# The value mix of two local attention phases, computed transposed on 64x64 parts of TensorE

## The chip, the cores and the metric

One Trainium2 chip, one of its cores. The metric is the time of one execution on the device in microseconds (us); lower is better. The kernel is written directly for the engines: TensorE (PE), VectorE (DVE), ScalarE (ACT), GpSimd (POOL) and SyncE (SP) each have a program of their own, and semaphores tie them together.

## The reference

A four-layer decoder over `x` (32 sequences of 64 tokens, 128 features) with attentions, cross attentions and feed-forward blocks. The change touches the local attention of `_L0_ffn_ref`, which is computed twice (depth 2), each time followed by a gated feed-forward block. With 64 tokens in a sequence and a window of 64, each sequence is one window, and it comes down to this:

```
qkv = shift_token(x) @ wqkv                      # 128 -> 3 * 512
q, k, v = heads of 64 features, 8 heads
q, k = rotary(l2norm(q) * q_scale), rotary(l2norm(k) * k_scale)
sim = einsum('bhid,bhjd->bhij', q * 8, k)        # 64 x 64 for each sequence and head
attn = softmax(where(causal, sim, -max), axis=-1)
out = einsum('bhij,bhjd->bhid', attn, v)
x = x + out.reshape(b, n, 512) @ wo
```

## The kernel before, in words

The 2048 token rows are 16 tiles of 128 rows (two sequences each). A turn takes two tiles, called streams 0 and 1, so a phase has 8 turns (`TURNS`). The two local attentions are the phases F0_ATTN and F1_ATTN. They run through `piped3` (L272): a body works on three turns at once, a tail (scores, softmax, mix, output), a middle (norms and rotation of queries and keys) and a front (load, transpose, projection). Each phase has two bodies without a tail, six full ones (tail, middle, front) in a hardware loop, a seventh tail without a front, and an eighth tail alone.

Every engine walks its part of `three` in the order in which it is written; there is no planner. For a full body:

- DVE (`three` of `wide_vector`, L1112): for the middle the sums of squares (L1045, L1048) and the scaling to unit length (L1052); for the tail the softmax shift (L378, L380); rotation of the middle's stream 0 (L1034 to L1036); for the tail the row sums (L1067), their reciprocals (L1072) and `normal_heads` (L1080), which reads the mixed heads of PSUM, multiplies them by one over the row sum and writes them to `mixed_heads`; rotation of stream 1; the residual sum (L335).
- PE (`three` of `wide_tensor`, L910): for the tail the transposes of queries and keys (L820), the values (L838), the scores (L813, 16 matmuls for a stream, on 64x64 parts of the array); for the front the transposes of `xs` (L304) and the projection (L827); then for the tail `turn_probs_pe` (L397: four transposes L401 for a stream, 128x128, two heads each), `mix` (L841), `turn_heads` (L850, four transposes L853), `output` (L857, four accumulating matmuls for a stream).
- ACT (`three` of `wide_scalar`, L995): queries (L954), values (L961, two copies for a stream), for the front L312 and L314, exp (L388), squares (L1011), the copy of the turned probabilities (L395) and of the turned heads (L969).
- POOL (`three` of `wide_pool`, L764): for the middle the power -1/2 (L768, twice), stage of `xs` (L299), L780, and for each stream the addition that completes the rotation (L783), as soon as DVE has rotated that stream.

The helper `mm` (L285) records all matmuls, so PE's matmuls show as L285 and are told apart by tiles and shapes. A float32 matmul has two records in the profile, a transpose one.

The mix multiplies, for head pair `c` and sequence `b`, the turned probabilities (128 rows: the keys of two heads; 64 columns: queries) by `values64`, which holds the values of both heads in block diagonal form with zeros between. Its result has queries in partitions, so `turn_heads` transposes it before `output`.

`mixed_heads` shares its memory with `probs`, `headsT` with `probsT`. All are parts of one SBUF tensor, `arena`, and PSUM shows as `ps`.

## Time and profile before

| | |
|---|---|
| time, median of 3 runs | 1894.24 us (1893.24 to 1895.31) |
| the profiled execution's own time | 1894.01 us |
| its span, first to last instruction | 1892.2 us |
| busy: PE, DVE, ACT, POOL | 78%, 64%, 42%, 39% |
| TensorE clock granted, mean | 0.896 of full speed |

The busy shares are means over 15 phases with different limits, and say little about the two phases that change. The timeline below lists merged instructions: start in the span, length from the first to the last of the group, engine, line, operands, count, and in square brackets how long the engine sat idle before and what ended that. "PE" rows are matmuls. The change applies to the stretches from 288 to 449 us and from 547 to 706 us.

### The profile page before, as it was taken

What the parts mean: (1) busy time and instruction counts of PE and PEld (TensorE: products, weight loads), DVE (VectorE), ACT (ScalarE), POOL (GpSimd) and SP (SyncE); (2) the same over time, 40 slices, a digit from 0 to 9 for tenths busy, and PEclk for the clock granted to TensorE, in tenths of its full rate; (3) what the DMA queues carried; (4) which work ended last, traced back from release to release, by engine and by line L of the source; (5) the groups of instructions that cost most, each with busy time, mean ns of one, the idle gap of its engine ahead of it and who ended that gap; (6) DMA issues with size and microseconds to landing.
All of it is one profiled execution on the core that took longest, in us unless ns stands there. A gap on an engine that the chain in (4) does not pass through costs nothing.

```text
span 1892.2 us, 42651 instructions
## 1 busy us (share of the span) xinstructions
PE 1479.7 (78%) x16082; PEld 1042.8 (55%) x16082; DVE 1216.5 (64%) x2671; ACT 789.4 (42%) x1513; POOL 730.5 (39%) x961
## 2 busy tenths in 40 slices
PE   4979967877878878799999786928988688898830
PEld 2656735556745556466666554925555567565520
DVE  4974658784467765657575586435788245698867
ACT  1542315554545544354545353514555123355520
POOL 2541125641155532324242362544566111356620
PEclk9988869998889997999999897868999599899975
DMA  7000000000000000000000000211000000000000
GB/s 297 0 1 0 0 1 1 0 1 19 0 1 0 0 6 6 17 1 0 0 0 0 1 0 23 50 52 77 0 1 1 0 1 0 1 0 2 0 2 22
DMA packets 14384, 27.69 MB, mean 15 GB/s; under 512 B 3830, under 2 KB 10998, under 8 KB 13544
## 3 DMA queue, kind: packets, MB, share of 16 engines
q1 hardware_dynamic: 13064, 24.15, 3.6%
q0 software_dynamic: 1248, 2.56, 0.6%
q8 instruction: 48, 0.79, 0.2%
q14 instruction: 24, 0.20, 0.0%
HBM read 23.10 MB, written 3.60 MB: 14 GB/s over the span
## 4 chain that ended last, share of the span: by engine, by line
PE 33%; issue 28%; DVE 17%; POOL 16%; ACT 4%; POOLq 1%; SPq 0%; DMA 0%; DVEq 0%; ACTq 0%
PE ps L285 27%; DVE maxima L378 6%; POOL arena L783 4%; DVE arena L380 3%; PE ps L401 3%; POOL inv_norm L768 3%; ACT arena L388 2%; POOL arena L754 2%; POOL arena L465 2%; DVE heads_out L677 2%; POOL arena L758 2%; POOL rstd L319 1%; PE ps L820 1%; DVE arena L1034 1%; POOL arena L1662 1%
## 5 line engine op out<-in xcount | busy, mean ns | idle before, releaser
L285 PE MATMUL ps<-arena 128*32 128x64 f32 (+6 forms) x7797 | 380.1, 281 | 45.0 <-ACT arena L395 11.8
L285 PEld LDWEIGHTS ps<-arena 64*64 64x64 f32 (+4 forms) x7797 | 252.7, 133 | 159.2 <-issue 98.5
L465 POOL TENSOR_TENSOR arena<-arena,w_const 128x1024 f32<-128x1024 f32 x96 | 182.3, 1901 | 151.1 <-DVE arena L662 64.9
L378 DVE TENSOR_REDUCE maxima<-ps 128x16 f32<-128x1024 f32 (+1 forms) x144 | 158.4, 1100 | 101.4 <-PE ps L285 100.1
L319 POOL TENSOR_TENSOR rstd<-var_eps,minus_half 128x1 f32<-128x1 f32 x160 | 87.7, 565 | 287.4 <-DVE var_eps L361 287.4
L388 ACT ACTIVATE arena<-arena 128x1024 f32<-128x1024 f32 (+1 forms) x144 | 138.5, 962 | 135.0 <-DVE arena L380 134.5
L401 PE MATMUL ps<-w_const,arena 128*128 128x128 f32 x1024 | 139.0, 280 | 46.9 <-ACT arena L388 46.7
L380 DVE TENSOR_TENSOR arena<-ps,maxima 128x1024 f32<-128x1024 f32 (+1 forms) x144 | 159.2, 1106 | 5.0
L401 PEld LDWEIGHTS ps<-w_const,arena 128*128 128x128 f32 x1024 | 115.9, 143 | 69.9 <-ACT arena L388 62.5
L395 ACT COPY arena<-ps 128x1024 f32<-128x1024 f32 (+1 forms) x144 | 129.6, 916 | 29.5 <-PE ps L401 28.7
L783 POOL TENSOR_TENSOR arena<-arena 128x1024 f32<-128x1024 f32 x32 | 77.2, 2413 | 135.4 <-DVE arena L1036 135.4
L677 DVE RECIPROCAL heads_out<-ps 128x128 f32<-128x128 f32 x96 | 91.3, 951 | 56.8 <-PE ps L285 56.5
L304 PE MATMUL ps<-w_const,xs 128*128 128x128 f32 x192 | 63.8, 341 | 79.4 <-POOL xs L299 69.9
L304 PEld LDWEIGHTS ps<-w_const,xs 128*128 128x128 f32 x192 | 28.3, 148 | 136.7 <-issue 69.8
L768 POOL TENSOR_TENSOR inv_norm<-sq_floor,minus_half 128x16 f32<-128x16 f32 x32 | 92.5, 2907 | 16.4 <-DVE sq_floor L1048 14.9
L617 ACT COPY arena<-ps 64x128 f32<-64x128 f32 x192 | 49.1, 256 | 114.4 <-PE ps L285 113.3
L954 ACT COPY arena<-ps 128x1024 f32<-128x1024 f32 x48 | 48.6, 1012 | 115.3 <-PE ps L820 115.3
L820 PE MATMUL ps<-w_const,arena 128*128 128x128 f32 x512 | 68.5, 281 | 25.9 <-POOL arena L783 20.2
L820 PEld LDWEIGHTS ps<-w_const,arena 128*128 128x128 f32 x512 | 56.9, 143 | 36.8 <-POOL arena L783 20.0
L961 ACT COPY arena<-ps 64x512 f32<-64x512 f32 (+1 forms) x96 | 69.3, 721 | 13.5 <-PE ps L285 11.3
L754 POOL TENSOR_TENSOR arena<-arena 128x1024 f32<-128x1024 f32 x16 | 37.4, 2355 | 95.8 <-DVE arena L1036 95.8
L1052 DVE TENSOR_TENSOR arena<-ps,inv_norm 128x1024 f32<-128x1024 f32 x32 | 39.2, 1224 | 52.5 <-POOL inv_norm L768 52.5
(280 smaller groups left out, 3090.7 us busy)
## 6 DMA issues: line engine op xcount, KB each, us to landing
experts<-in_pack_moe SPq DMA_DIRECT2D x2, 4180.0 KB, 19.8
w_a<-in_pack_a SPq DMA_DIRECT2D x1, 2080.0 KB, 16.9
w_fa<-in_pack_fa SPq DMA_DIRECT2D x2, 1024.0 KB, 11.5
moe_out<-arena SPq DMA_DIRECT2D x5, 256.0 KB, 2.3
w_fg<-in_pack_fg SPq DMA_DIRECT2D x2, 537.0 KB, 11.8
ctxT<-in_ctxT SPq DMA_DIRECT2D x1, 1024.0 KB, 7.5
moe_in<-state SPq DMA_DIRECT2D x1, 1024.0 KB, 5.5
out<-state SPq DMA_DIRECT2D x1, 1024.0 KB, 5.1
```

The source lines that it names most:

```text
L285: return nc.tensor.matmul(o, lhsT, rhs, start=start, stop=stop, skip_group_check=True)
L319: nc.gpsimd.tensor_tensor(rstd[s][:, :], var_eps[s][:, :], minus_half[:, 0:1], ALU.pow)\
L378: nc.vector.reduce_max(mx, sc, X_AXIS).then_inc(signal["max_ready"], 1)
L380: nc.vector.tensor_tensor(probs(s)[:, 0:heads * S].rearrange("p (a h k) -> p a h k", a=2, h=half), sc, mx.unsqueeze(3).broadcast_to([P, 2, ...
L388: nc.scalar.activation(probs(s)[:, 0:n], probs(s)[:, 0:n], ACT.Exp, scale=scale)\
L395: nc.scalar.copy(probsT(s)[:, 0:n], pair(s, 2)[:, 0:n]).then_inc(signal["probsT_ready"], 1)
L401: last = nc.tensor.transpose(pair(s, 2)[:, j * P:(j + 1) * P], probs(s)[:, j * P:(j + 1) * P], ident)
L465: nc.gpsimd.tensor_tensor(keys_wide(s).rearrange("p (b h t) -> p b h t", b=SEQS, h=8), key8(s).rearrange("p (b t) -> p b t", b=SEQS).unsqu ...
L677: nc.vector.reciprocal(heads_out[s][:, :], bank(s, 1, P, 2 * P)).then_inc(signal["sums_inverted"], 1)
L768: nc.gpsimd.tensor_tensor(inv_norm[s][:, :], sq_floor[s][:, :], minus_half[:, :], ALU.pow).then_inc(signal["norms_inv"], 1)
L783: nc.gpsimd.tensor_tensor(roped(s), roped(s), rope_swapped(s), ALU.add)\
L820: last = nc.tensor.transpose(pair(s, first)[:, j * P:(j + 1) * P], source[:, j * P:(j + 1) * P], ident)
```

## The change

It replaces three steps of the tail in both phases:

- `normal_heads` goes. `normal_probs` on DVE multiplies the probabilities in `probs` by one over their row sums, in place, before they are turned. `turn_probs_pe` now waits for that (`heads_normal`) where it waited for exp (`probs_ready`).
- `mix` becomes `mix_turned`: for every pair `c`, sequence `b` and head `par` of the pair one matmul with the 64x64 block of values as the stationary side and the turned probabilities as the moving side. It reads partitions `par*64` to `par*64+63` and writes the same partitions of PSUM bank 2. The result has features in partitions, so it needs no transpose: `turn_heads` and its four transposes for a stream go, and `heads_mixed` on ACT copies PSUM to `headsT` (the counterpart of L969).
- The values are kept densely in `values_plain`, one copy (`values_whole`) for a stream in place of two (L961).

The third wide phase, L1_ATTN, keeps the old functions.

```diff
-                        turn_probs_pe(tail, heads)
-                        for s in STREAMS:
-                            mix(tail, s)
-                    if tail:
-                        for s in STREAMS:
-                            turn_heads(tail, s)
+                        turn_probs_pe(tail, heads, ready="heads_normal")
+                        for s in STREAMS:
+                            mix_turned(tail, s)
                         for s in STREAMS:
                             output(tail, s)
...
+                def mix_turned(t, s):
+                    t.wait("probsT_ready", s, alone=True)
+                    for c in range(half):
+                        for b in range(SEQS):
+                            for par in range(2):
+                                rows, cols = slice(par * S, (par + 1) * S), slice(c * P + b * S, c * P + (b + 1) * S)
+                                last = mm(bank(s, 2)[rows, cols], values_plain(s)[rows, b, c, :],
+                                          probsT(s)[rows, cols])
+                    last.then_inc(signal["mixed"], 1)
...
+        def values_plain(s):
+            return probsT(s)[:, 512:1024].rearrange("p (b c d) -> p b c d", b=SEQS, c=4)
...
+                def values_whole(t):
+                    for s in STREAMS:
+                        t.wait("v_projected", s)
+                        nc.scalar.copy(values_plain(s).rearrange("p b c d -> p (b c d)"), bank(s, 2))\
+                            .then_inc(signal["values_ready"], 1)
+
+                def heads_mixed(t):
+                    for s in STREAMS:
+                        t.wait("mixed", s)
+                        nc.scalar.copy(headsT(s)[:, 0:half * P], bank(s, 2)).then_inc(signal["headsT_ready"], 1)
...
+                def normal_probs(t):
+                    for s in STREAMS:
+                        t.wait("sums_inverted", s)
+                        per_head = probs(s)[:, 0:heads * S].rearrange("p (h k) -> p h k", h=heads)
+                        nc.vector.tensor_tensor(per_head, per_head,
+                                                inv_sum[s][:, 0:heads].unsqueeze(2).broadcast_to([P, heads, S]),
+                                                ALU.mult).then_inc(signal["heads_normal"], 1)
...
                     if tail:
                         row_sums(tail)
-                        normal_heads(tail)
+                        normal_probs(tail)
                     if middle:
                         unit_rotated(middle, 1, tail)
```

PE's program in the loop body of F0_ATTN, from the turned probabilities to the loop's end, first before (L401 transposes of probabilities, `arena 64x128` the mix, L853 transposes of heads, `w_fa,arena` the output):

```order
L401 MATMUL ps<-w_const,arena 128x128 [waits probs_ready]
L401 MATMUL ps<-w_const,arena 128x128 x3
L285 MATMUL ps<-arena 64x128 [waits probsT_ready]
L285 MATMUL ps<-arena 64x128 x7
L285 MATMUL ps<-arena 64x128 [waits probsT_ready]
L285 MATMUL ps<-arena 64x128 x7
L853 MATMUL ps<-w_const,arena 128x128 [waits heads_normal]
L853 MATMUL ps<-w_const,arena 128x128 x3
L285 MATMUL ps<-w_fa,arena 128x128 [waits headsT_ready]
L285 MATMUL ps<-w_fa,arena 128x128 x3
```

and after the change:

```order
L401 MATMUL ps<-w_const,arena 128x128 [waits heads_normal]
L401 MATMUL ps<-w_const,arena 128x128 x3
L401 MATMUL ps<-w_const,arena 128x128 [waits heads_normal]
L401 MATMUL ps<-w_const,arena 128x128 x3
L285 MATMUL ps<-arena 64x64 [waits probsT_ready]
L285 MATMUL ps<-arena 64x64 x15
L285 MATMUL ps<-arena 64x64 [waits probsT_ready]
L285 MATMUL ps<-arena 64x64 x15
L285 MATMUL ps<-w_fa,arena 128x128 [waits headsT_ready]
L285 MATMUL ps<-w_fa,arena 128x128 x3
```

The wait for DVE's multiplication stood behind the mix; it now stands ahead of the transposes of probabilities, and the mix has 16 matmuls for a stream in place of 8.

DVE's program in the same body, before:

```order
L1067 TENSOR_REDUCE row_sum<-arena 128x8 [waits probs_ready] x2
L1072 RECIPROCAL inv_sum<-row_sum 128x8 [waits sums_ready]
L1080 TENSOR_TENSOR arena<-ps,inv_sum 128x512 [waits sums_inverted,mixed] x2
L1034 TENSOR_TENSOR arena<-arena,rope_f 128x1024 [waits q_turned]
L335 TENSOR_TENSOR inner<-state,ps 128x128
```

and after (L1087 and L1092 are L1067 and L1072 of before, L1054 is L1034):

```order
L1087 TENSOR_REDUCE row_sum<-arena 128x8 [waits probs_ready] x2
L1092 RECIPROCAL inv_sum<-row_sum 128x8 [waits sums_ready]
L1099 TENSOR_TENSOR arena<-arena,inv_sum 128x512 [waits sums_inverted] x2
L1054 TENSOR_TENSOR arena<-arena,rope_f 128x1024 [waits q_turned]
L335 TENSOR_TENSOR inner<-state,ps 128x128
```

The multiplication keeps its place and its size. It no longer waits for PE's mix, and reads SBUF (`arena`) where it read PSUM (`ps`).

## Rows read from the trace of the kernel before

**Rows 1.** Timeline, DVE, one full body of F0_ATTN (350.0 to 370.4 us).

```profile
350.00 1.22 DVE L1045 TENSOR_REDUCE sq_sum<-arena 128x16 f32<-128x1024 f32 x1
351.26 0.40 DVE L1048 TENSOR_SCALAR sq_floor<-sq_sum 128x16 f32<-128x16 f32 x1
...
357.55 1.22 DVE L1052 TENSOR_TENSOR arena<-ps,inv_norm 128x1024 f32<-128x1024 f32 x1 [1.65 <-POOL inv_norm L768]
...
364.87 0.32 DVE L1072 RECIPROCAL inv_sum<-row_sum 128x8 f32<-128x8 f32 x2
365.73 0.69 DVE L1080 TENSOR_TENSOR arena<-ps,inv_sum 128x512 f32<-128x512 f32 x1 [0.54 <-PE ps L285]
366.60 0.69 DVE L1080 TENSOR_TENSOR arena<-ps,inv_sum 128x512 f32<-128x512 f32 x1 [0.18 <-PE ps L285]
...
370.02 0.29 DVE L335 TENSOR_TENSOR inner<-state,ps 128x128 f32 x1 [0.20 <-PE ps L285]
370.44 1.22 DVE L1045 TENSOR_REDUCE sq_sum<-arena 128x16 f32<-128x1024 f32 x1
```

**Rows 2.** Timeline, POOL, ACT and PE, the same body.

```profile
349.26 2.36 POOL L783 TENSOR_TENSOR arena<-arena 128x1024 f32<-128x1024 f32 x1 [3.49 <-DVE arena L1036]
351.74 5.78 POOL L768 TENSOR_TENSOR inv_norm<-sq_floor,minus_half 128x16 f32<-128x16 f32 x2
353.85 2.41 ACT L961 COPY arena<-ps 64x512 f32<-64x512 f32 x4
356.64 0.69 PE L285 MATMUL ps<-arena 64*64 64x64 f32 x32
359.06 3.60 PE L285 MATMUL ps<-w_fa,shT 128*128 128x512 f32 x8
363.84 2.37 POOL L783 TENSOR_TENSOR arena<-arena 128x1024 f32<-128x1024 f32 x1 [5.38 <-DVE arena L1036]
364.58 1.97 PE L285 MATMUL ps<-arena 128*64 128x128 f32 x32 [1.05 <-ACT arena L395]
366.48 0.66 PE L853 MATMUL ps<-w_const,arena 128*128 128x128 f32 x4
367.18 0.59 ACT L969 COPY arena<-ps 128x512 f32<-128x512 f32 x1 [2.15 <-PE ps L853]
367.84 2.03 PE L285 MATMUL ps<-w_fa,arena 128*128 128x128 f32 x16
```

**Rows 3.** Timeline, POOL and DVE, a body without a tail (283 to 287 us).

```profile
283.49 3.26 POOL L783 TENSOR_TENSOR arena<-arena 128x1024 f32<-128x1024 f32 x1 [2.73 <-DVE arena L1036]
284.46 2.84 DVE L1035 TENSOR_TENSOR arena<-arena,rope_f 128x512 f32<-128x512 f32 x1
```

**Rows 4.** Groups by shape, 268 to 460 us: count, busy us, mean ns, idle before.

```profile
L285 PE MATMUL ps<-arena 64*64 64x64 f32 x512 | 11.1, 224 | 0.0
```

**Rows 5.** Timeline, F1_ATTN: DVE's reduction and POOL's power that follows it.

```profile
566.58 1.22 DVE L1045 TENSOR_REDUCE sq_sum<-arena 128x16 f32<-128x1024 f32 x1 [0.26 <-issue]
568.09 5.78 POOL L768 TENSOR_TENSOR inv_norm<-sq_floor,minus_half 128x16 f32<-128x16 f32 x2 [0.38 <-DVE sq_floor L1048]
```

**Rows 6.** Stretches: length; PE, PEld, DVE, ACT, POOL busy; clock; DMA share; GB/s.

```profile
418.60:421.90 3.30, 0.10 (x8) 0.00 (x0) 3.01 (x4) 0.46 (x1) 0.69 (x3) 1.00 0.02 5
422.00:425.30 3.30, 2.98 (x16) 2.25 (x18) 3.27 (x5) 1.87 (x4) 0.16 (x1) 0.50 0.01 2
```

**Rows 7.** Timeline, PE, the seventh tail of F0_ATTN and the start of the eighth.

```profile
422.12 1.12 PE L401 MATMUL ps<-w_const,arena 128*128 128x128 f32 x4 [3.42 <-ACT arena L388]
...
424.49 3.68 PE L285 MATMUL ps<-arena 128*64 128x128 f32 x32
...
433.82 1.06 PE L820 MATMUL ps<-w_const,arena 128*128 128x128 f32 x8 [1.14 <-POOL arena L783]
```

**Rows 8.** Timeline, DVE, the eighth tail of F0_ATTN (438 to 449 us).

```profile
442.31 0.32 DVE L1072 RECIPROCAL inv_sum<-row_sum 128x8 f32<-128x8 f32 x2
...
449.31 0.29 DVE L335 TENSOR_TENSOR inner<-state,ps 128x128 f32<-128x128 f32 x1 [0.61 <-PE ps L285]
```

More of the change, by code:

```diff
@@ L395, in probsT_scalar, with turn_probs_pe @@
                 nc.scalar.copy(probsT(s)[:, 0:n], pair(s, 2)[:, 0:n]).then_inc(signal["probsT_ready"], 1)
-        def turn_probs_pe(t, heads, streams=STREAMS):
+        def turn_probs_pe(t, heads, streams=STREAMS, ready="probs_ready"):
             for s in streams:
-                t.wait("probs_ready", s)
+                t.wait(ready, s)
                 for j in range(heads // 2):
@@ L997, in three @@
                         queries(tail, 2)
-                        values(tail, 2)
+                        values_whole(tail)
                     if front:
@@ L1013, in three @@
                         probsT_scalar(tail, heads)
-                    if tail:
-                        heads_turned(tail)
+                        heads_mixed(tail)
                 if ph == L1_ATTN:
```

2 lines of the change are left out of this document (1 added, 1 removed).

## The prediction

> **What bounds the kernel now.** I read the timeline of one full body first, since only twelve bodies (six in each of two phases) and four closing tails change; then the same stretch of the other engines; then the places where an engine met what the change will meet.
>
> A full body takes 370.44 - 350.00 = 20.44 us [rows 1]. The reader should see a closed ring. POOL finishes its addition for stream 1 at 349.26 + 2.36 = 351.62; the small DVE step L1048, begun at 351.26, lasts 0.40 and ends just then; POOL's two powers run from 351.74 to 357.52 and release L1052 at 357.55 [rows 1, 2]. From there DVE works without a gap to the reciprocals, done at 364.87 + 0.32 = 365.19, waits 0.54 and 0.18 for the mix around L1080, rotates stream 1 and so releases POOL's next addition [rows 1]. So DVE and POOL set the body. PE is close behind: DVE's second residual sum waits 0.20 for the output and starts at 370.02, and DVE's next reduction stands behind it in program order [rows 1]. That second path, from the multiplication to the residual sum, is the one that the change rebuilds.
>
> **The change, step by step, in that body.** Up to 365.19 nothing moves.
>
> *Removed from DVE: the wait for the mix*, 0.54 + 0.18 = 0.72 us [rows 1]. This is what the change could gain.
>
> *The multiplication itself* keeps 0.69 us [rows 1], if it can start. It has now two inputs in SBUF, and POOL's addition for stream 0 runs from 363.84 to 366.21 [rows 2]. The trace shows what such a pair does to each other: L1035, also with two SBUF inputs, 128x512, took 2.84 us beside POOL's addition and ended at 287.30, 0.55 after POOL's 286.75, and POOL's own took 3.26 instead of 2.36 [rows 2, 3]. L1080, which reads PSUM, ran beside that addition in 0.69 [rows 1, 2]. So I take the first multiplication to end at 366.21 + 0.55 = 366.76 and the second 0.60 later, 367.36. Bounds: without the hindrance 365.88 and 366.49, which is 0.9 earlier. The Trainium skill ("SBUF — State Buffer", section "SBUF: two separate sides") says that VectorE with two SBUF inputs and GpSimd hold one pair of ports in turn, each for a whole instruction. The trace agrees. The gain of 0.72 is so taken back: the rotation of stream 1 starts at about 367.3 against 367.2 now.
>
> *Transposes of probabilities.* They stood in the shadow of the row sums; now they wait for the multiplication. Distances from the present chain: PE starts 0.06 after DVE (366.42 to 366.48), four transposes take 0.66, ACT starts 0.04 later and its copy of 128x512 takes 0.59 [rows 1, 2]. Stream 1: transposes 367.42 to 368.08, copy 368.12 to 368.71. Stream 0 is 0.6 ahead.
>
> *The mix.* No row has 64x64 matmuls on two parts of the array. The nearest is the score: 32 records over four parts in 0.69 us, one record alone 0.224 [rows 2, 4], so one record every 15 ns and one for each part every 60 ns. Over two parts I take one in 30 ns: 31 x 0.030 + 0.22 = 1.16 us for a stream. Bounds: 0.69 (as the score), and 1.97 (the two parts never overlap, 31 x 0.060 + 0.22 = 2.1; the present mix of both streams together takes 1.97 [rows 2]). Stream 0 starts at 368.16, stream 1 follows at 369.12 and ends at 370.28; its last copy ends at about 370.9.
>
> *Transposes of heads and their wait* go: eight transposes, 1.3 us of PE; the same count of transposes of probabilities stands in their place on this path, so it gains nothing.
>
> *Output.* 16 records take 2.03 us [rows 2], and PE starts them behind the whole mix, at about 370.1 against 367.84 now. They end at 372.1, and with the 0.15 that DVE needs now (369.87 to 370.02) the second residual sum starts at 372.3, against 370.02.
>
> *The values.* Four copies, 2.41 us, become two of 0.59 [rows 2]. I cost this gain of 1.2 us of ACT at nothing: the score ends at 357.33, before the powers release L1052 (357.55) [rows 1, 2]. That cover stays.
>
> *What the next body makes of it.* The reduction starts 0.42 after the second sum [rows 1], at 372.7. Where POOL is free, its power follows 1.51 behind the reduction (566.58 to 568.09) [rows 5], at 374.2, against 351.74 + 20.44 = 372.18. So a body grows by 2.0 to 2.1 us with TensorE at full clock. With a mix of 0.69, and no hindrance, it would still be 2.1 - 0.9 - 0.6 = 0.6.
>
> *The clock.* PE ends the projection at 362.66 [rows 2] and has nothing until 366.82: a hole of 4.2 us that the transposes fill today. In the seventh tail PE idles 3.42 us; the granted clock there is 1.00 (2.4 GHz) during the idle stretch and 0.50 (1.2 GHz) in the next, where four transposes take 1.12 (0.66 at full clock) and the mix 3.68 (1.97) [rows 2, 6, 7]. The new hole is longer, and it is followed by the very work on the path. At the low level throughout, the second stream's transposes end 0.9 later and the mix takes about 1.7 to 2.0 more: 2.7 us. If the clock stays up it is 0. The drop may begin only during the transposes and end before the output, so I take 1.8, nearer to the upper end since no hole of that length here keeps the clock.
>
> *Sum.* A full body: 2.1 + 1.8 = 3.9; twelve: 46.8. Seventh tail: PE is at the low level already; multiplication, transposes and mix in line end about 3.8 later (my estimate, as for a full body); PE idles 1.14 ahead of the eighth tail's second transposes, for POOL [rows 7], and that much is absorbed: +2.7. Eighth tail: from the reciprocals' end (442.63) to the second sum (449.31) now 6.7 [rows 8]; new 1.3 for two multiplications (POOL idle), 4.9 for the rest as above, 1.8 for the clock: 8.0, +1.4. Both phases: 8.2. Total 46.8 + 8.2 = 55 us on the profiled execution's 1894.0, which lies 0.2 from the median: **1949 us**.
>
> **Rivals.**
>
> 1. *Full clock.* The hole is there but the clock is not lowered, or only outside the path. Then twelve bodies of 2.1 and small ends (+4): 1894 + 29 = 1923. For it: bodies in the trace with short PE holes keep 1.00. Against: rows 6.
> 2. *Nothing in the way but the longer chain.* The multiplication starts at once beside POOL, and the mix is as fast as the score: 12 x 0.6 + 2 = +9, 1903. Against: rows 3.
> 3. *The two parts serialize.* The mix takes 2.1 for a stream. Only its whole excess (2 x 0.95) comes on the path: up to +1.9 for a body, +27 in all, 1975. The two parts differ in rows and write the same bank at once. The Trainium skill ("TensorEngine Tiling (Array Packing)", "Gotcha 1: PSUM Pressure") says that different row tiles cannot access one bank at the same time; by that rule the sum is this rival's. The present score writes one bank from one row part at a time for eight pairs of matmuls, so no row decides it.
> 4. *The other side: faster.* The chain behind the multiplication fits under DVE's rotation of stream 1, so the ring of DVE and POOL keeps the turn and the wait of 0.72 is gained: 12 x 0.72 + about 3 at the ends = 12, 1882. It decides at one point: the second output must be done 3.5 us after the second multiplication (366.5 to 370.0, no hindrance). My chain needs 4.9, of which output alone is 2.0 and two copies and transposes 1.8, all from rows. For it: less PE work and one DVE wait fewer. Against: every hop has its row.
>
> That the change does not do what it says has little room: DVE's multiplication loses its wait in its program, and PE's wait moves ahead.
>
> **How the numbers follow.** Forecast (hindrance and lowered clock, 1935 to 1962): 0.62. Full clock 0.17, serial parts 0.08, longer chain alone 0.05, faster 0.08. The range 1908 to 1966 takes in the forecast's own, the full clock with a shorter mix (12 x 1.5 + 3 gives 1915) and part of the serial case. A measurement of this kernel tells 0.2% (3.8 us) from no change. Faster by more: 0.08; within: 0.02; slower: 0.90.
>
> **What would show it.** In the changed profile's timeline: bodies of about 24 us; the first multiplication L1099 ending 0.55 behind POOL's addition, near 1.5 us long; PE idle some 4 us ahead of L401; a granted clock of 0.50 over the transposes and the mix; about 3 to 4 us idle on DVE ahead of the second L335; POOL's power released by L1048's successor and no longer back to back with the addition. I am wrong if bodies stay near 20.4 or fall: then the chain is shorter than its hops. If L1099 takes 0.69 at once, the hindrance was wrong; if L401 and the mix run at 1.00, the clock term was.

## The result, and the profile after

The changed kernel takes 1958.43 us (median of 4 runs, 1944.97 to 1960.52); the kernel before, beside it, 1893.74 us (4 runs, 1884.47 to 1895.31). The ratio is 1.033, with a 95% interval of 1.030 to 1.037: 65 us slower. The forecast was 1949 us, 55 more than the profiled execution before, and the likeliest case's range (1935 to 1962) holds the result.

The profiled execution took 1960.52 us (span 1958.4). From its page, the group of all transposes of probabilities, whose idle time ahead is 109.5 us (46.9 in the kernel before) and now ends mostly with DVE's multiplication L1099:

```profile
L401 PE MATMUL ps<-w_const,arena 128*128 128x128 f32 x1024 | 147.1, 290 | 109.5 <-DVE arena L1099 73.5
```

A full body of F0_ATTN in the timeline of the changed kernel (start, length, engine, line, operands, count, idle before and its releaser). It answers to [rows 1, 2]:

```profile
359.44 1.22 DVE L1065 TENSOR_REDUCE sq_sum<-arena 128x16 f32<-128x1024 f32 x1
...
360.95 5.78 POOL L771 TENSOR_TENSOR inv_norm<-sq_floor,minus_half 128x16 f32<-128x16 f32 x2 [3.51 <-DVE sq_floor L1068]
...
373.05 2.34 POOL L786 TENSOR_TENSOR arena<-arena 128x1024 f32<-128x1024 f32 x1 [5.37 <-DVE arena L1056]
...
374.31 2.23 DVE L1099 TENSOR_TENSOR arena<-arena,inv_sum 128x512 f32<-128x512 f32 x2
...
376.00 1.72 PE L401 MATMUL ps<-w_const,arena 128*128 128x128 f32 x8 [4.12 <-DVE arena L1099]
...
377.64 3.12 PE L285 MATMUL ps<-arena 64*64 64x64 f32 x64
...
382.01 0.29 DVE L335 TENSOR_TENSOR inner<-state,ps 128x128 f32 x1 [3.13 <-PE ps L285]
...
382.90 0.29 DVE L335 TENSOR_TENSOR inner<-state,ps 128x128 f32 x1 [0.61 <-PE ps L285]
383.32 1.22 DVE L1065 TENSOR_REDUCE sq_sum<-arena 128x16 f32<-128x1024 f32 x1
```

The body takes 383.32 - 359.44 = 23.88 us where it took 20.44. The two multiplications take 2.23 in all (in the trace the first has 1.63, the second 0.68, 0.08 of it overlapping). The first ends 0.55 behind POOL's addition (373.05 + 2.34 = 375.39; 374.31 + 1.63 = 375.94). PE was idle for 4.12 ahead of the transposes, and DVE for 3.13 ahead of the first residual sum. POOL's powers start 1.51 behind the reduction and are no longer back to back with POOL's addition.

Stretches of the same body (length; PE, PEld, DVE, ACT, POOL busy; granted clock; DMA share; GB/s), for the hole, transposes, mix and output:

```profile
371.90:376.00 4.10, 0.01 (x1) 0.01 (x1) 4.10 (x8) 1.36 (x2) 2.34 (x1) 1.00 0.00 0
376.00:377.60 1.60, 1.60 (x8) 1.13 (x8) 1.60 (x3) 0.59 (x1) 0.00 (x0) 0.67 0.00 0
377.60:380.70 3.10, 3.10 (x66) 2.99 (x65) 1.28 (x3) 1.17 (x2) 1.74 (x1) 0.62 0.00 0
380.70:382.70 2.00, 2.00 (x22) 2.00 (x19) 0.29 (x1) 0.58 (x1) 0.61 (x1) 1.00 0.00 0
```

The clock is at its upper level (1.00, 2.4 GHz) in the hole, falls to the lower one (0.50, 1.2 GHz) in the transposes, and is up again for the output. The means of 0.67 and 0.62 say that a part of each stretch ran at either level.

Two bodies of the changed kernel keep the clock over this work, the second and the third of F1_ATTN. The second:

```profile
603.45 6.19 PE L285 MATMUL ps<-w_fa,shT 128*128 128x512 f32 x8
609.38 2.24 DVE L1099 TENSOR_TENSOR arena<-arena,inv_sum 128x512 f32<-128x512 f32 x2
611.07 1.26 PE L401 MATMUL ps<-w_const,arena 128*128 128x128 f32 x8 [1.43 <-DVE arena L1099]
612.50 2.08 PE L285 MATMUL ps<-arena 64*64 64x64 f32 x64 [0.17 <-ACT arena L395]
...
616.73 0.29 DVE L335 TENSOR_TENSOR inner<-inner,ps 128x128 f32 x1 [0.62 <-PE ps L285]
```

There the low level falls on the projection (6.19 us in place of 3.60), which the path does not wait for here; it leaves a hole of 1.43 us, and from the end of the second multiplication (611.62) to the second sum it takes 5.11 us, against 6.36 in the body above. I call such a body one "at full clock", since the work on its path is.

**Where the time went.** I take the start of each second residual sum L335 of a turn, eight in a phase, and compare the two traces. The table gives the seven lengths between them in order: five full bodies, then the seventh and the eighth tail.

| | before | after |
|---|---|---|
| F0_ATTN | 20.43 x5, 20.94, 17.48 | 23.85, 23.86, 23.87, 23.89, 23.89, 23.79, 16.89 |
| F1_ATTN | 21.83, 20.43 x4, 20.97, 15.67 | 22.64, 22.62, 23.79, 23.77, 23.79, 23.73, 16.89 |
| last sum of F0 / of F1 at | 449.31 / 706.22 | 471.36 / 751.32 |
| from there to the span's end | 1186.0 | 1207.1 |

So +45.1 us have come together by the end of F1_ATTN: about 22 in F0_ATTN, 2 in the feed-forward phase between, 21 in F1_ATTN. **Another 21.1 us lie in stages whose code the change does not touch.** They show in PE's clock, not in the work. The first row of each pair is the stretch right behind F1_ATTN, the second the second mixture-of-experts stage. Before:

```profile
706.20:871.30 165.10, 137.13 (x1075) 101.78 (x1076) 98.64 (x279) 71.89 (x147) 51.92 (x68) 0.91 0.03 8
...
1449.10:1584.40 135.30, 105.59 (x829) 81.87 (x825) 56.81 (x139) 34.42 (x74) 24.69 (x52) 0.81 0.00 1
```

After:

```profile
751.30:923.90 172.60, 148.43 (x1075) 111.71 (x1076) 98.85 (x279) 71.77 (x147) 51.90 (x68) 0.84 0.03 8
...
1503.80:1651.70 147.90, 117.98 (x825) 92.27 (x824) 56.71 (x139) 34.17 (x73) 24.58 (x51) 0.73 0.00 0
```

The number of PE's instructions is the same (a few records are missing), DVE's, ACT's and POOL's busy times are the same, but PE is busy for 11.3 and 12.4 us more at a granted clock of 0.84 in place of 0.91, and 0.73 in place of 0.81. These two stretches make 20.1 of the 21.1 us. How much of this belongs to the change is taken up with after_again below.

### The profile page after: what moved, and what is told of

Its sections match the earlier page's. It is cut to its first block, busy times and chain, and to the rows that moved or that the text cites. A ratio compares the mean times of both kernels' runs of the same rounds, so it can differ in the third digit from the quotient of the medians.

```text
span 1958.4 us, 43348 instructions
## 1 busy us (share of the span) xinstructions
PE 1498.3 (77%) x16451; PEld 1070.1 (55%) x16466; DVE 1226.7 (63%) x2671; ACT 772.2 (39%) x1481; POOL 730.6 (37%) x961
## 4 chain that ended last, share of the span: by engine, by line
PE 32%; issue 30%; DVE 17%; POOL 14%; ACT 4%; POOLq 1%; DMA 1%; SPq 0%; DVEq 0%; ACTq 0%
PE ps L285 27%; DVE maxima L378 5%; POOL inv_norm L771 3%; DVE arena L380 3%; PE ps L401 3%; ACT arena L388 2%; POOL arena L786 2%; POOL arena L757 2%; POOL arena L465 2%; DVE heads_out L677 2%; POOL arena L761 2%; POOL rstd L319 1%; DVE arena L1054 1%; POOL arena L1690 1%; POOL xs L299 1%
## 5 line engine op out<-in xcount | busy, mean ns | idle before, releaser
L285 PE MATMUL ps<-arena 64*64 64x64 f32 (+7 forms) x8309 | 391.1, 278 | 34.0 <-DVE state L367 9.9
L285 PEld LDWEIGHTS ps<-arena 64*64 64x64 f32 (+5 forms) x8309 | 267.0, 138 | 149.2 <-issue 103.4
L401 PE MATMUL ps<-w_const,arena 128*128 128x128 f32 x1024 | 147.1, 290 | 109.5 <-DVE arena L1099 73.5
L401 PEld LDWEIGHTS ps<-w_const,arena 128*128 128x128 f32 x1024 | 119.6, 147 | 137.1 <-DVE arena L1099 86.0
L285 PE MATMUL ps<-w_fa,shT 128*128 128x512 f32 x128 | 73.0, 724 | 0.8 <-ACT shT L314 0.8
L285 PE MATMUL ps<-xT,w_fg 128*128 128x128 f32 (+1 forms) x384 | 69.6, 353 | 5.1 <-ACT xT L1256 5.0
L823 PE MATMUL ps<-w_const,arena 128*128 128x128 f32 x512 | 66.3, 282 | 8.0 <-POOL arena L786 4.3
L1072 DVE TENSOR_TENSOR arena<-ps,inv_norm 128x1024 f32<-128x1024 f32 x32 | 39.2, 1224 | 51.5 <-POOL inv_norm L771 51.5
## 6 DMA issues: line engine op xcount, KB each, us to landing
experts<-in_pack_moe SPq DMA_DIRECT2D x2, 4180.0 KB, 19.5
w_a<-in_pack_a SPq DMA_DIRECT2D x1, 2080.0 KB, 17.2
```

What stands on the lines that cost most here:

```text
L285: return nc.tensor.matmul(o, lhsT, rhs, start=start, stop=stop, skip_group_check=True)
L401: last = nc.tensor.transpose(pair(s, 2)[:, j * P:(j + 1) * P], probs(s)[:, j * P:(j + 1) * P], ident)
```

## The experiments

My theory after reading the trace: at full clock a body is 2.2 us longer because the dependency multiplication, transposes, mix, output now ends last (2.73 us from the second multiplication's end, 367.29, to the second sum, 370.02, in the kernel before by [rows 1]; 5.11 now); 0.95 of that is the hindrance of the multiplication by POOL's addition, and the lowered clock adds 1.2. Rivals: the new mix itself is slow; the wait is not what costs; the layout costs elsewhere.

The kernels ran in three sessions on different chips, each beside the kernel before, whose median was 1911.0 (first), 1910.1 (second) and 1894.0 us (third). Ratios go by the session's own. A ratio takes in all stages that no edit touches, and these differ by more than some of the effects sought, so I read an effect from the bodies and from the last column first. Bodies and last column come from one profiled execution; in e_order and e_warm that was the fastest of its runs, 17 and 14 us under the median.

| kernel | us, median | ratio to before (95%) | full bodies, us | last sum of F1 at |
|---|---|---|---|---|
| e_port | 1948.0 | 1.017 (1.014 to 1.020) | 21.68 and 23.0 to 23.2 in turn | 736.0 |
| e_warm | 1954.5 | 1.023 (1.020 to 1.026) | 22.62 to 24.7, mostly 23.41 | 742.6 |
| e_port_warm | 1942.4 | 1.014 (1.011 to 1.018) | 21.72 and 23.41, one 24.26 | 736.6 |
| e_nowait | 1918.9 | 1.003 (1.002 to 1.005) | 20.49 | 705.0 |
| e_oldmix | 1968.4 | 1.032 (1.028 to 1.035) | 23.75, one 24.87 | 765.4 |
| e_order | 1933.2 | 1.014 (1.011 to 1.017) | 21.06, 21.37 and 22.5 | 719.2 |
| b_order | 1929.1 | 1.012 (1.009 to 1.015) | 21.35, 22.7 and 23.9 | 721.9 |
| b_shift | 1912.6 | 1.001 (0.999 to 1.003) | 20.43 | 709.0 |
| after_again | 1956.2 | 1.032 (1.030 to 1.035) | 22.63 and 23.78 | 748.3 |
| e_order_warm | 1926.3 | 1.017 (1.013 to 1.021) | 21.10 | 720.2 |
| e_ahead | 1870.5 | **0.986 (0.984 to 0.989)** | 18.30 | 674.5 |
| b_ahead | 1936.7 | 1.020 (1.017 to 1.023) | 23.3 to 24.5 | 748.1 |

### e_nowait: the wait alone taken away

```diff
-                        turn_probs_pe(tail, heads, ready="heads_normal")
+                        turn_probs_pe(tail, heads)
...
-                        nc.vector.tensor_tensor(per_head, per_head,
+                        nc.vector.tensor_tensor(aside, per_head,
```

> The changed kernel, but PE turns the probabilities as soon as exp is done, so they are not divided by their sums; DVE's multiplication stays, with its result written beside them where nobody reads it. All other steps as in the changed kernel, the 64x64 mix included. The division is left out of what is computed in both phases. Theory: the chain starts at the projection's end, PE has no hole and keeps clock 1.00, the output is ready while DVE still rotates stream 1, so the body falls to the ring of DVE and POOL: about 20.4 plus 0.2 (the hindered multiplication), and the time to about 1894 plus or minus 10. Rival (the 64x64 mix costs the time): body stays above 22.

This kernel leaves the division out of what it passes on. Timeline of one body: the mix now starts ahead of the multiplication, and the sums follow DVE.

```profile
385.20 2.08 PE L285 MATMUL ps<-arena 64*64 64x64 f32 x64 [1.13 <-ACT arena L395]
...
385.63 2.24 DVE L1100 TENSOR_TENSOR arena<-arena,inv_sum 128x512 f32<-128x512 f32 x2
...
390.13 0.47 DVE L335 TENSOR_TENSOR inner<-state,ps 128x128 f32 x2
```

Bodies of 20.49 against 20.43 before. With the same new mix, the same two multiplications (2.24 us, hindered all the same), and no wait between them and the transposes, the loss of 3.4 us is gone. The place of the wait is the cause; the new layout by itself costs nothing. It gains nothing either, since here too the ring of DVE and POOL ends last: the 0.72 us that DVE no longer waits for the mix are given back to the hindrance. The whole kernel stays 7.9 us above the kernel before of its session (1918.9 against 1911.0). This lies behind the changed phases, since its last sum of F1_ATTN comes 1.2 us earlier than in the kernel before (705.0 against 706.2).

### e_port: the multiplication ahead of POOL's addition

```diff
                             middle.wait("q_parts", s)
+                            if tail and s == 0:
+                                tail.wait("heads_normal", 1, alone=True)
                             nc.gpsimd.tensor_tensor(roped(s), roped(s), rope_swapped(s), ALU.add)
```

> The changed kernel; POOL adds stream 0's rotation only when both multiplications of the probabilities are done, so no addition of POOL's runs beside them. In the changed kernel a full body takes 23.86 us, and the first multiplication ends some 1.0 us late. Theory (hindrance by POOL, longer chain, lowered clock): the two multiplications take 1.3 us together instead of 2.23, everything behind them comes 0.9 earlier, a body takes about 22.9, twelve bodies give 11 us: about 1947. Rival (POOL does not matter, the multiplication is slow by itself or hidden): body stays within 0.2 of 23.86, time about 1958. A second rival: the granted clock changes its place with the shift, and the body moves by something other than 0.9.

Timeline of one body at full clock, POOL and DVE:

```profile
371.90 1.29 DVE L1101 TENSOR_TENSOR arena<-arena,inv_sum 128x512 f32<-128x512 f32 x2
...
373.33 3.21 POOL L788 TENSOR_TENSOR arena<-arena 128x1024 f32<-128x1024 f32 x1 [8.06 <-DVE arena L1101]
374.24 2.84 DVE L1057 TENSOR_TENSOR arena<-arena,rope_f 128x512 f32<-128x512 f32 x1
...
378.29 0.29 DVE L335 TENSOR_TENSOR inner<-state,ps 128x128 f32 x1 [0.41 <-PE ps L285]
```

The two multiplications take 1.29 in place of 2.23, and the body 21.68 in place of 22.63 at full clock: **the hindrance is worth 0.95 us a body**. Every second body has 23.0 to 23.2, with the mix at the low clock (3.3 to 3.6 us); the bodies of 21.68 have the low level on the projection instead (4.8 to 6.4 us). I had expected 22.9 for all; the mean is 22.2, so the second rival (the clock changes its place) had a part in the gain of 15 us by the end of F1_ATTN. It has not vanished, it has moved: POOL's addition now takes 3.21 beside DVE's L1057, which takes 2.84 (0.68 alone), as in [rows 3]. There it ends before the output. The chain from the end of the second multiplication to the second sum is 378.29 - 373.19 = 5.10, as in the changed kernel at full clock (5.11).

### e_warm, e_port_warm: matmuls with unused results in PE's hole

```diff
                     if tail:
+                        for s in STREAMS:
+                            tail.wait("probs_ready", s, alone=True)
+                            for _ in range(2):
+                                mm(bank(s, 2), ident, part(w, "wqk")[:, 0:512])
                         turn_probs_pe(tail, heads, ready="heads_normal")
```

> The changed kernel; four float32 matmuls of 512 columns with a result that nobody reads fill PE's hole between the projection and the transposes of the probabilities (they write PSUM banks that the transposes overwrite). Theory: the granted clock stays at 1.00 through transposes and mix; the transposes take 1.2 us instead of 1.72 and the mix of both streams 2.0 to 2.3 instead of 3.12, so a body falls from 23.86 by 1.2 to 1.5 to about 22.4, and the time by about 16 us to 1942. Rival (the mix is slow because the two parts of the array serialize, the clock has little part): mix stays near 3 us at full clock, body falls by less than 0.6, time 1951 or more.

> Both edits, POOL's later addition and the filled hole. Theory: the gains add, body near 21.5, time about 1930; what is left over the 20.44 of the kernel before is the length of the chain itself (multiplication, transposes, copy, mix, copy, output). Since the multiplication ends 0.9 earlier the filler may now delay the transposes by up to 0.5, so 21.5 to 22.0. Rival (the chain at full clock fits under DVE's rotation): body at 20.4 or less.

Timeline of one body of e_warm, and its stretch from transposes to output:

```profile
368.15 5.30 PE L285 MATMUL ps<-w_fa,shT 128*128 128x512 f32 x8
...
374.19 2.25 DVE L1103 TENSOR_TENSOR arena<-arena,inv_sum 128x512 f32<-128x512 f32 x2
...
376.72 1.04 PE L401 MATMUL ps<-w_const,arena 128*128 128x128 f32 x8
...
378.09 2.08 PE L285 MATMUL ps<-arena 64*64 64x64 f32 x64 [0.33 <-ACT arena L395]
...
382.31 0.29 DVE L335 TENSOR_TENSOR inner<-state,ps 128x128 f32 x1 [0.60 <-PE ps L285]
```

```profile
376.00:384.00 8.00, 7.57 (x107) 6.52 (x105) 4.59 (x8) 3.18 (x6) 2.35 (x1) 1.00 0.00 0
```

The clock is 1.00 over transposes, mix and output, and the mix takes 2.08 in place of 3.12. Filling the hole keeps the clock: that part of the theory holds. But the expected body of 22.4 and time were missed. The low level now falls on the projection in most bodies (5.30 us here in place of 3.60, with a granted clock of 0.61 over its first 3.4 us), behind PE's other hole (2.18 and 0.77 us ahead of the transposes of `xs`), so the filler starts late, ends behind the multiplication (376.44 here, transposes at 376.72), and the chain has 5.87 in place of 5.10. The body follows the projection: 22.62 where that takes 3.60, which is the changed kernel's body at full clock, 23.41 with 5.3, 24.7 with 6.5. In e_port_warm it is 21.72 with 3.60, 23.41 with 5.3 and 24.26 with 6.0 (expected 21.5 to 22.0). So the filler fits its hole, just, and the low clock in front of it is what makes it late; a shorter one would leave more room, which was not tried.

### e_oldmix: the wait, but with the old mix and its transposes of heads

```diff
-                            mix_turned(tail, s)
+                            mix(tail, s)
+                        for s in STREAMS:
+                            tail.wait("copied_out", s)
+                            for j in range(half):
+                                last = nc.tensor.transpose(pair(s, 2)[:, j * P:(j + 1) * P],
+                                                           mixed_heads(s)[:, j * P:(j + 1) * P], ident)
+                            last.then_inc(signal["heads_turned"], 1)
...
-                        values_whole(tail)
+                        values(tail, 2)
...
+                            nc.scalar.copy(mixed_heads(s)[:, 0:half * P], pair(s, 2)[:, 0:half * P])
```

> Half of the change: probabilities divided ahead of their transposes, but the old mix with its block diagonal values; ACT copies its result to SBUF, the transposes of heads and their copy stay. Against the changed kernel this has one more copy (0.6), one more set of transposes (0.7) and about the same time in the mix (1.97 against 2.08 at full clock). Theory (the wait ahead of the transposes is the loss and the transposed mix is a gain of 1.3 or more for a body): body about 25.3, time 17 us or more above the changed kernel. Rival (the 64x64 mix is the loss): body at or below 23.9.

```profile
379.00 2.24 DVE L1109 TENSOR_TENSOR arena<-arena,inv_sum 128x512 f32<-128x512 f32 x2
...
380.69 1.26 PE L401 MATMUL ps<-w_const,arena 128*128 128x128 f32 x8 [2.52 <-DVE arena L1109]
...
383.92 1.41 PE L950 MATMUL ps<-w_const,arena 128*128 128x128 f32 x8
...
387.46 0.29 DVE L335 TENSOR_TENSOR inner<-state,ps 128x128 f32 x1 [0.60 <-PE ps L285]
```

In the timeline of one body the chain holds transposes (1.26), mix (1.97), transposes of heads (1.41) and output, and from the second multiplication to the second sum it takes 6.23, 1.13 more than the 5.10 of the new mix. I had expected 25.3 us, with the clock as low as in the changed kernel; the bodies have 23.75, since here the clock stays at 1.00 over the chain in the steady bodies: the projection, partly at the low level (5.1 us in place of 3.6), ends later and leaves PE a hole of only 2.52 in place of 4.12. So the new layout does shorten the path, by 1.13 us a body at full clock, and the changed kernel gives that back where its clock falls (23.8). The body of 23.75 also meets the number that I had set for the rival that the 64x64 mix is the loss (23.9 or less). It does not speak for it: at the same clock the new mix has the shorter chain, and e_nowait has the same mix in bodies of 20.49. By the last sum of F1_ATTN, at 748 to 751 us against 765, the old mix is still the slower one; the ratios of the two, taken in different sessions, do not part them.

### e_order, b_order, e_order_warm: another order on DVE

Rotation of stream 0 moves between the two scalings, where DVE waits for POOL's powers [rows 1]. Then POOL's addition is over before the multiplication. The same edit went into the changed kernel (e_order) and the kernel before (b_order); e_order_warm adds a filler behind the score.

```diff
                     for s in STREAMS:
+                        if s == 1:
+                            unit_rotated(t, 0, last)
                         t.wait("norms_inv", s)
...
-                    if middle:
-                        unit_rotated(middle, 0, tail)
```

```diff
                             if middle:
-                                middle.wait("unit_ready", s)
+                                middle.wait("unit_ready", s, alone=True)
+                                for k in range(0 if s else 5):
+                                    mm(bank(s, 1), ident, part(w, "wqk")[:, 0:512])
```

> The changed kernel; DVE rotates stream 0 of the middle between the two scalings to unit length, where it now idles 1.65 us for POOL's power, in place of behind the softmax. Row sums and multiplication then follow the softmax at once, and no addition of POOL's runs beside the multiplication. Theory (the chain behind the multiplication is what counts; it costs 5.11 us at full clock): in a body, scaling of stream 1 moves 0.7 later, the second multiplication ends 14.8 us after the body's start (16.9 in the changed kernel), PE's hole shrinks from 4.1 to about 1 us and the clock stays at 1.00; the second sum starts at 14.8 + 5.1 = 19.9, body 20.3. Twelve bodies give 12 x 3.5 = 42 us over the changed kernel, so about level with the kernel before (ratio 0.99 to 1.00). Rival (the transposed mix is a loss in any order): bodies stay above 21.5.

> The kernel before with the same move on DVE. There the mix and all behind it hang on PE's projection, which follows the scaling of stream 1, and that comes 0.7 later. Theory: the second sum still starts 7.4 us behind the projection's end, so a body takes 20.43 + 0.6 = about 21.0, time 7 us above the kernel before. Rival (DVE's own work sets the body, so filling its gap pays): body 19.0 to 19.8, 8 to 17 us faster.

> The changed kernel with the rotation of stream 0 between the two scalings, and five matmuls of 512 columns (results unused) on PE behind the score, in the hole of 2.4 us ahead of the projection of the next tiles. Theory (what separated that order from its expected 20.3 us was the projection at the low clock, 4.9 us for eight records in place of 3.6, which held up ACT's activations and with them the copy of transposed probabilities): projection 3.6 us, chain from the second multiplication to the second sum 5.1, bodies 20.4 to 20.6, ratio 0.998 to 1.005. Rival (the order itself costs it): bodies stay 21.0 to 21.4 with the clock up, ratio 1.010.

e_order, timeline of one body and two stretches:

```profile
362.45 4.88 PE L285 MATMUL ps<-w_fa,shT 128*128 128x512 f32 x8
...
366.24 1.28 DVE L1101 TENSOR_TENSOR arena<-arena,inv_sum 128x512 f32<-128x512 f32 x2
...
367.36 1.02 ACT L1032 ACTIVATE arena<-ps 128x1024 f32<-128x1024 f32 x1 [0.69 <-PE ps L285]
...
373.23 0.29 DVE L335 TENSOR_TENSOR inner<-state,ps 128x128 f32 x1 [0.60 <-PE ps L285]
```

```profile
358.00:360.40 2.40, 0.00 (x0) 0.00 (x0) 2.26 (x4) 0.00 (x0) 2.40 (x3) 1.00 0.00 0
...
362.40:364.40 2.00, 2.00 (x4) 0.97 (x4) 1.93 (x4) 1.15 (x3) 1.46 (x1) 0.50 0.00 0
```

The hindrance is gone (1.28), as expected, but I had not expected what follows. The scaling of stream 1, for which PE's second transpose of `xs` waits, now comes 1 us later, and with it the projection. So PE's hole lies ahead of the projection, and has grown there. The projection meets the low clock (4.88 to 6.3 us), ACT's activation L1032 waits for it and stands in front of ACT's copy of the turned probabilities: the chain is 5.70 to 7.2 in place of 5.10. Bodies of 21.06, 21.37 and 22.5, not 20.3. In b_order the same late projection stands in front of the transposes of probabilities themselves: its bodies are 21.35 where the projection keeps 3.60 (I had expected 21.0), 22.7 with 5.3 and 23.9 with 6.4, and the ratio is 1.012 where I had expected 7 us, 1.004. The rival, 19.0 to 19.8, fell.

e_order_warm, where the projection keeps its clock (3.70), timeline of one body:

```profile
378.15 4.53 PE L285 MATMUL ps<-w_fa,w_const 128*128 128x512 f32 x10 [0.42 <-DVE arena L1076]
```

In this run the projection keeps its clock, but I mis-sized the filler: five float32 matmuls are ten records of 0.43, 4.53 us in a hole of 2.4. The projection ends at 387.10, late again, and all bodies have 21.10. That is the rival's number (21.0 to 21.4 with the clock up), so this run alone doesn't decide. One body of e_order speaks against the rival, the first of F1_ATTN, where the projection keeps its clock and comes in time:

```profile
555.69 1.23 DVE L1074 TENSOR_TENSOR arena<-ps,inv_norm 128x1024 f32<-128x1024 f32 x1 [1.63 <-POOL inv_norm L771]
...
561.00 3.60 PE L285 MATMUL ps<-w_fa,shT 128*128 128x512 f32 x8
...
571.28 0.29 DVE L335 TENSOR_TENSOR inner<-inner,ps 128x128 f32 x1 [0.62 <-PE ps L285]
```

The chain has 5.10 there, and from the first scaling to the second sum it takes 15.59 us, against 16.20 (from 357.03) in the body of 21.06 above. By this such a body would take 20.45 (my estimate, 21.06 - 0.61), near the 20.3 expected; no run has it as its steady state.

### e_ahead and b_ahead: the next tiles' sums of squares ahead of the residual sums

On top of the order above, DVE takes the reductions and floors for the next body while it waits for the output:

```diff
                         unit_rotated(middle, 1, tail)
+                    if front:
+                        norms(front)
                     if tail:
                         finish(tail)
```

> The changed kernel with the rotation of stream 0 between the scalings, and with the sums of squares of the next tiles (reduction and floor, 2.8 us of DVE) taken ahead of the residual sums, where DVE waits for the output. Theory (the body is a ring: second sum, reduction, two powers on POOL, scaling, and back through multiplication, transposes, mix and output; the reduction and part of the powers can leave it): POOL's first power starts as POOL's second addition ends, about 2.8 us earlier; bodies 17.5 to 18.5, twelve of them 50 to 70 us under the changed kernel's, ratio to the kernel before 0.975 to 0.985. Rival (PE becomes the bound, with 14.4 to 14.7 us of work a body and its waits, or the low clock moves into the mix): bodies 19.5 to 20.5, ratio 0.995 or more.

> The kernel before with the same two moves on DVE (rotation of stream 0 between the scalings, the next tiles' sums of squares ahead of the residual sums). Theory (the ring is the same, but the heads must be multiplied behind the mix, and rotation of stream 1 stands behind that on DVE): bodies 18.5 to 19.5, half a microsecond to one and a half longer than in the changed kernel with the same moves; ratio 0.98 to 0.99. Rival (the old mix, whose transposes of probabilities need no multiplication, is again the faster of the two): bodies equal to or under those of the other, ratio under 0.98.

e_ahead, timeline of one body:

```profile
374.59 1.30 DVE L1067 TENSOR_SCALAR sq_floor<-sq_sum 128x16 f32<-128x16 f32 x1
...
375.97 5.78 POOL L771 TENSOR_TENSOR inv_norm<-sq_floor,minus_half 128x16 f32<-128x16 f32 x2
...
377.17 0.48 DVE L335 TENSOR_TENSOR inner<-state,ps 128x128 f32 x2
```

POOL's powers start ahead of the residual sums, not 1.9 behind the last one. The bodies fall to 18.30, and the kernel takes **1870.5 us, 1.4% under the kernel before** (0.984 to 0.989) and 4.4% under the changed kernel of its session (1870.5 / 1956.2). The bodies are as expected, the ratio of 0.986 just misses the 0.985. Against e_order, which lacks only this move, that is 2.8 to 4.2 us (2.15 against the 20.45 estimated above): the ring through reduction and powers was what turned the longer chain into a longer body. The floor step, 0.17 alone, takes 1.30 beside POOL's addition and holds the residual sums back; that is still to be had.

b_ahead, timeline of one body:

```profile
378.63 2.03 PE L285 MATMUL ps<-w_fa,arena 128*128 128x128 f32 x16
...
380.34 1.21 DVE L1044 TENSOR_REDUCE sq_sum<-arena 128x16 f32<-128x1024 f32 x1
...
384.16 0.48 DVE L335 TENSOR_TENSOR inner<-state,ps 128x128 f32 x2
```

With the old layout the same edit costs: 23.3 to 24.5 us, where I had expected 18.5 to 19.5. The output is done at 380.66, but the sums stand behind the norms until 384.16. The old mix has DVE's idle time ahead of its multiplication (the mix ends late), and nothing left behind it; the norms were put into the wrong gap. So this run does not say what the old layout can reach with them in the right one, which was not tried.

### b_shift and after_again: what the unchanged stages do by themselves

b_shift is the kernel before with three writes of unused buffers at the start of F0_ATTN:

```diff
+                if ph == F0_ATTN:
+                    for idle in (probs(0), probs(1), probsT(0)):
+                        nc.vector.memset(idle, 0.0)
```

> The kernel before with three writes of 128x1024 zeros by DVE to unused memory at the start of F0_ATTN, so that all behind it begins some 2 us later. Theory (part of the changed kernel's loss comes from stages that it doesn't touch, since the clock's low stretches fall elsewhere in them): full bodies stay at 20.4, while the time behind the second attention phase, 1186.0 us in the kernel before and 1207.1 in the changed one, comes out different by more than 3 us in one direction or the other. Rival (unchanged stages take the same time whenever they start): it stays within 2 us of 1186, and the total grows by 2 us.

> The changed kernel unaltered, once more, beside the kernel before on the same chip, so that the trials can be set against it. Theory (the loss is made of body lengths that the order of the work fixes, and the times of the unchanged stages drift from one loading to the next): bodies of 23.8 to 23.9 us with the clock low over transposes and mix, 22.6 where it stays up, ratio 1.025 to 1.035. Rival (the distance of the first measurement was partly chance): ratio 1.020 or less with the same bodies; what stands behind the second changed phase then takes 1195 us or less in place of 1207.

after_again repeats the ratio and its bodies, as expected, 1.032 (1.030 to 1.035), with 22.63 and 23.78. Behind F1_ATTN it takes 1198.0, against 1207.1 and 1186.0. Stretches behind F1_ATTN and of the second mixture-of-experts stage, in after_again:

```profile
748.30:920.90 172.60, 148.44 (x1075) 111.76 (x1076) 98.89 (x279) 71.76 (x147) 51.95 (x68) 0.84 0.03 8
1500.90:1639.30 138.40, 109.06 (x825) 84.14 (x824) 56.80 (x140) 34.18 (x73) 24.57 (x51) 0.80 0.00 1
```

The first stretch is the same to the last digit (172.60), so +7.5 there comes again with this kernel; of the 12.6 in the second stretch only 3.1 do. The two profiles are not of like executions: the first (1960.52) lies 2 us above the median of its four, whose fastest took 1944.97; that of after_again is the fastest of its four (1948.43, the others 1953.31 to 1960.08). So executions of one kernel part by up to 15 us, and the 12 us behind F1_ATTN in this profile are probably a low reading, the 21 of the first the more usual one. In b_shift it takes 1201.4 behind F1_ATTN, more than 3 us away from 1186.0, as the theory wanted; but most of that is a stage that is longer in every kernel of its session, so the forecast's number is met for another reason. Beside the kernel before of its own session b_shift is 2.5 us slower (1912.6 against 1910.1, interval of the ratio 0.999 to 1.003), which is what the rival said. What speaks for the theory is the first stretch alone, 161.80 against 165.10, and the two are of different sessions. The longer stage, before and in b_shift:

```profile
1129.20:1258.30 129.10, 92.64 (x944) 80.91 (x944) 60.46 (x141) 49.80 (x135) 51.42 (x64) 0.79 0.15 37
```

```profile
1130.90:1279.50 148.60, 96.91 (x944) 84.62 (x944) 60.41 (x141) 49.75 (x135) 50.03 (x64) 0.75 0.13 32
```

It takes 145 to 149 us in the profiles of all eight kernels of the first two sessions, and 129 to 130 in the other six profiles. Most of it is not PE's work (4.3 us more), and its size is about that of the 17 us by which the kernel before is slower in those sessions. So it goes with the chip or the session for the most part; which of the two, and why, is open (two of the first session's 14 executions of the kernel before, at 1894.57 and 1896.87, had the lower time even there).

## Why the prediction was right, and where its terms were off

- **What bounds the kernel** (the ring of DVE and POOL, with the path from multiplication to residual sum close behind): right. e_nowait cuts the one dependency and the body returns to 20.49; e_ahead shortens the ring and it falls to 18.30. Of the 3.4 us that a body gained, e_port takes out 0.95 for the hindrance, the clock is 1.2 (23.85 against 22.63), and the rest, 1.25, is the longer chain.
- **The multiplication** hindered by POOL's addition, 0.9: measured 0.95 (1.63 against 0.68), and e_port takes exactly that out of the body. It ends 0.55 behind the addition, as [rows 3] said.
- **The mix**, 1.16 for a stream: 1.15 in the trace at full clock. Two streams take 2.08, 64 records, so one record every 33 ns. Parts that never overlap would need 60 ns a record by [rows 2, 4], 3.8 us. The third rival fell. Its rule (the Trainium skill, "TensorEngine Tiling (Array Packing)", "Gotcha 1: PSUM Pressure") is not borne out here: two parts with different rows write different partitions of one bank side by side.
- **The chain** from the second multiplication to the second sum, 4.9: 5.10.
- **The body at full clock**, +2.1: 22.63 against 20.43, +2.2.
- **The clock term**, 1.8: this is the term that was mis-sized. It measured 1.2 (23.8 to 23.9 against 22.63), and nothing in the second and third body of F1_ATTN (in after_again of F0_ATTN too), where the low level falls on the projection. I had costed the low level at +0.9 for the transposes and +1.7 to 2.0 for the mix, and taken two thirds of it. The eight transposes lost 0.46 (1.72 for 1.26) and the mix 1.04 (3.12 for 2.08), at granted clocks of 0.67 and 0.62, together 1.50, of which 1.25 reached the chain (6.36 against 5.11); the rest lies under the wait for ACT's copies. The clock was back at 1.00 before the mix had ended. The prediction said that this could be, and still took too much.
- **Twelve bodies**, 46.8: they made 36.8 (2.6 and 4.0 in the first bodies of the two phases, their approach included, 17.2 and 13.1 in the five behind), mostly by that term.
- **The tails**, 8.2: 6.2 in sum. The seventh gave +2.85 and +2.76 (forecast +2.7). The eighth gave -0.6 and +1.2 (forecast +1.4 each); before it had 17.48 in one phase and 15.67 in the other, and I had read only the slow one. The +1.4 is also a slip by 0.1: 8.0 less 6.7 is 1.3.
- **The sum**, 55: 45 in the changed phases and the one between, and 21 in stages that I had costed at nothing without naming them. An overrated clock term and an unseen cost outside partly cancelled, so it is luck that the total (+66 in span) is nearer to the forecast than its parts are. With the 45 alone it would have been 1939, still in the range.
- Rival 1 (full clock, 1923) holds for two or three bodies of a phase, not for a phase. Rival 2 needed no hindrance and a mix of 0.69, and had neither. Rival 4 (faster) named its point: the second output within 3.5 us after the second multiplication. It takes 5.1.

What stays open: why some 10 us more come again with the changed kernel in the 430 us behind F1_ATTN (both of its profiles have them: 172.6 and 260.8 to 261.1 where the kernel before has 165.1 and 257.9). In the first of these stretches PE runs at a clock of 0.84 in place of 0.91. So it does in e_port, e_nowait and e_order_warm (172.5 to 172.7 us), while e_ahead, but also b_order, b_ahead and e_oldmix with the old mix, have 169.0 to 169.4 at 0.87, so the mix alone does not set it. e_warm and e_order have 163.8 and 163.3, but their profiles are of unusually fast executions. No run isolates what sets it, nor says how much of it changes from one execution to the next.

## What to carry to other kernels

A step that leaves a chain may lengthen it by its new place: dividing the probabilities ahead of their transposes put PE, ACT, PE, ACT, PE behind one multiplication (5.11 us to the second sum) where the old order had PE, ACT, PE (2.73 us). Count what stands between the moved step and the next thing that its own engine needs, not the work saved. And once a longer latency is there, fill it: with the norms of the next tiles in DVE's idle time the new layout became the fastest version measured. That the old layout could not reach as much is not shown, since b_ahead put them into the wrong gap.

## What the runs showed of the hardware

- DVE's steps with two inputs in SBUF and POOL's addition hindered each other, and whichever came second lost: multiplication 1.63 for 0.68, rotation 2.84 for 0.68, POOL's addition 3.21 for 2.35. It reaches a step of 16 columns with one tensor input: the floor L1067 took 1.30 for 0.17 and ended as the addition did (e_ahead). The row sums beside the addition were not hindered (1.27 for two, with it in the changed kernel and without it in e_port). The powers of POOL did not do this to the scaling and rotation beside them (e_order, 1.23 each).
- After a hole of 4.12 us on PE the clock fell over the transposes and the mix in every body of the changed kernel that has such a hole; after 1.43 and 2.49 it stayed up, after 2.43 it fell. Moving a hole moves the victim: transposes and mix in the changed kernel, the projection in e_order and e_warm. Matmuls with unused results keep the clock up (mix 2.08 for 3.12), and pay only where they end before the work that they protect.
- The same unchanged code behind F1_ATTN took 1186 to 1213 us in fourteen profiles, 16 to 20 of it in one stage that is longer in two of the sessions. A change's cost read from its own phases and the cost on the whole time can part by 20 us in 1900.
